# A graph, attention and expert network on one core: first expert layer scattered by token, key loads placed behind the first stores of scoring

## The reference, cut to what matters

```python
# layer 0, graph: attention over edges
x_l = x @ W_l + b_l;  x_r = x @ W_r + b_r
alpha = einsum(leaky_relu(x_r[dst] + x_l[src]), att) + log(edge_weight)
out = segment_softmax(alpha, dst) applied to x_l[src], summed by dst
...
# layer 0, experts: the two best of eight per token, summed without weights
logits = h @ Wg + bg
top2 = two largest experts of each token
y = sum over e in top2 of (gelu(h @ W1[e] + b1[e]) @ W2[e] + b2[e])
# layer 1: graph convolution (project, gather by src, sum by dst), attention, experts with capacity
```

## Time and profile before

| | us |
|---|---|
| median of three runs (5753.02 to 5766.75) | 5758.02 |
| the profiled execution | 5764.05 |
| its span in the trace | 5762.3 |
| planning (0 to 86.9) | 86.9 |
| projecting (to 248.9) | 162.0 |
| scoring (to 1395.4) | 1146.5 |
| normalising (to 1512.1) | 116.7 |
| aggregating, attention (to 2090.2) | 578.1 |
| routing of layer 0 (to 2339.1) | 248.9 |
| experts of layer 0 (to 2821.9) | 482.8 |
| combining (to 2990.7) | 168.8 |
| all of layer 1 (to 5762.3) | 2771.6 |

### The profile page before, as it was taken

One profiled execution on the slowest core, in us unless ns is written; L12 is line 12 of the kernel. 1 busy time (PEld: TensorE's weight loads), 2 busy tenths in 40 slices (PEclk: granted clock), 3 DMA queues, 4 the chain that ended last, 5 costly groups with the idle time before them and its releaser, 6 DMA issues. The chain is left out here.

```text
span 5762.3 us, 68520 instructions
## 1 busy us (share of the span) xinstructions
PE 3544.4 (62%) x13636; PEld 2691.9 (47%) x13637; DVE 2995.2 (52%) x6650; ACT 1002.2 (17%) x2108; POOL 3048.8 (53%) x2954
## 2 busy tenths in 40 slices
PE   3755556554399760599635555554555555583998
PEld 3633334333277550377534444443544545461665
DVE  5367777777899762144453444444333333442443
ACT  0022222221399510122110000000000000021111
POOL 1167777774288525100367777776777777503111
PEclk9867777776699875799755666665555555556999
DMA  5477777774288542521241111112111111122220
GB/s 199 96 208 231 234 231 229 236 230 148 88 272 271 171 158 72 166 64 64 79 114 32 32 33 32 33 33 42 32 33 32 32 33 33 24 74 83 95 74 31
DMA packets 430920, 630.36 MB, mean 109 GB/s; under 512 B 100204, under 2 KB 307838, under 8 KB 429383
## 3 DMA queue, kind: packets, MB, share of 16 engines
q1 hardware_dynamic: 298907, 375.58, 20.5%
q0 software_dynamic: 107056, 200.91, 14.7%
q10 hardware_dynamic: 24876, 53.00, 2.6%
HBM read 419.56 MB, written 222.20 MB: 111 GB/s over the span
## 5 line engine op out<-in xcount | busy, mean ns | idle before, releaser
L1846 POOL DMA_INDIRECT big<-t_d,src_tiles x1564 | 1493.0, 955 | 551.0 <-issue 463.0
L2069 PE MATMUL v_bank<-big,v_oh 128*128 x3328 | 682.9, 391 | 928.1 <-POOLq L1842 857.3
L2069 PEld LDWEIGHTS v_bank<-big,v_oh 128*128 128x128 f32 x3328 | 650.3, 299 | 1004.0 <-issue 1004.0
L642 POOL DMA_INDIRECT big<-xl_d,src_steps x832 | 833.2, 1001 | 302.6 <-issue 244.7
L1924 DVE TENSOR_TENSOR big<-big,v_bank 128x64 f32 x1664 | 367.7, 221 | 1148.4 <-PE v_bank L2069 914.3
L738 PE MATMUL se_z_ps<-big,se_oht 128*128 x1664 | 654.1, 553 | 482.0 <-DVE se_z L685 174.1
L738 PEld LDWEIGHTS se_z_ps<-big,se_oht 128*128 128x128 f32 x1664 | 424.6, 272 | 711.1 <-issue 623.8
L685 DVE TENSOR_TENSOR se_z<-se_z_ps,big 128x528 f32<-128x528 f32 x416 | 291.7, 701 | 353.9 <-DMA big<-xl_d,src_steps 284.2
L955 POOL TENSOR_TENSOR ae_v<-ae_v,ex 128x1792 f32<-128x1792 f32 x104 | 334.5, 3219 | 236.6 <-DMA ae_v<-xj_d 236.3
L996 PE MATMUL ae_bank<-ae_v,ae_oh 128*128 128x266 f32 x1664 | 402.9, 397 | 49.7 <-DVE big L980 37.1
L996 PEld LDWEIGHTS ae_bank<-ae_v,ae_oh 128*128 128x128 f32 x1664 | 310.1, 191 | 142.3 <-DVE big L980 53.3
(11 more groups left out here) (401 smaller groups left out, 5174.4 us busy)
## 6 DMA issues: line engine op xcount, KB each, us to landing
xj_d<-big SPq DMA_DIRECT2D x208, 528.0 KB, 3.2
ae_v<-xj_d SPq DMA_DIRECT2D x208, 528.0 KB
se_dlb<-dlr_d SPq DMA_DIRECT2D x104, 256.0 KB, 5.0
big<-t_d,src_tiles POOLq DMA_INDIRECT x1564
buf_d<-e_blank ACTq DMA_DIRECT2D x4, 4112.0 KB, 36.2
e_xs<-buf_d SPq DMA_DIRECT2D x106, 128.0 KB
y_d<-e_y SPq DMA_DIRECT2D x106, 128.0 KB
big<-xl_d,src_steps POOLq DMA_INDIRECT x832
```

The source lines that it names most:

```text
L642: nc.gpsimd.indirect_dma_start(half_of(u)[:, k, :], None, table, bass.IndirectOffsetOnAxis(ap=m.src[:, t:t + 1], axis=0)).then_inc(landed[ ...
L1846: nc.gpsimd.indirect_dma_start(rows[:, t % RING, :], None, table, bass.IndirectOffsetOnAxis(ap=m.srct[:, t:t + 1], axis=0)).then_inc(lande ...
L2069: last = nc.tensor.matmul(bank[u][:, k * MH:(k + 1) * MH], oh[:, u, k, :], of_block(rows, at[k]), start=True, stop=True)
```

## The change

In the planning stage the table reads are left out and made at the start of `project_nodes`; the nine weight loads go from SP in `project_nodes` to ACT in `edge_steps`, ahead of the zero fill. In scoring each of the first four stores is followed by four key loads, and TensorE reads the blocks of four steps at a time. The blank rows of `buf1_d` are written in `normalise_edges`, by SP, together with the padding rows of `y0_d`. A row of `buf0_d` has two more numbers: the token and its first expert. `experts0` compares the first expert with the tile's expert (`erow`) and so gets the row of `y0_d`, which now has two planes of NP = 6272 rows in token order; POOL scatters each tile of results there. Rows that hold no token carry 1e6 and are dropped. Combining reads both planes with plain loads, `m.back` is gone.

```diff
@@ edge_steps, SP and ACT
-                sp.wait_ge(stored, 64)
-                sp.dma_start(m.btab, m.btab_d[0:NS].rearrange("(a n) -> a n", a=1)).then_inc(stored, 16)
...
                 sp.wait_ge(floats, 4)
-                sp.dma_start(m.dlr_d.rearrange("(j p) e -> p j e", p=P), flb[:, :, :]).then_inc(stored, 16)
-                sp.wait_ge(stored, 128)
+                sp.dma_start(m.dlr_d.rearrange("(j p) e -> p j e", p=P), flb[:, :, :]).then_inc(rowed, 16)
+                sp.wait_ge(rowed, 16)
...
+                load_projections(act, m, a)
@@ score_edges, SP and PE
-                for c in range(CH):
-                    sp.dma_start(key[c * H:(c + 1) * H, :], kd[c].partition_broadcast(H)).then_inc(s["keys"], 16)
+                def load_keys(h, u, r):
+                    if isinstance(h, int) and h < 4:
+                        for c in range(h * CH // 4, (h + 1) * CH // 4):
+                            sp.dma_start(key[c * H:(c + 1) * H, :], kd[c].partition_broadcast(H)).then_inc(s["keys"], 16)
...
-                pipeline(sp, 2 * NG, 4, (0, load_locals), (4, store))
+                pipeline(sp, 2 * NG, 4, (0, load_locals), (4, store), (4, load_keys))
...
-                    blocks = blocks_of(nc, m, mybir.EngineType.PE, q * 2, 2)
+                    if v % 2 == 0:
+                        blocks[:] = blocks_of(nc, m, mybir.EngineType.PE, q * 2, 4)
@@ normalise_edges
+                for q in range(NE * CT // 16):
+                    sp.dma_start(slots[q], blank[:, :, :].to_broadcast([P, 16, RW])).then_inc(s["blanked"], 16)
+                for e in range(2):
+                    sp.dma_start(m.y0_d[e * NP + N:(e + 1) * NP, :], blank[0:NP - N, 0, 0:D]).then_inc(s["blanked"], 16)
@@ route, layer 0
+                    c.did(V.tensor_scalar(first[:, :], m.tmp1[:, :], float(NE), None, ALU.add))
...
-                    if v % 7 == 0 and layer == 1:
+                    if v % 7 == 0:
+                        for at, what in ((RW - 2, m.prob), (RW - 1, token)) if layer == 1 else ((TW - 2, token), (TW - 1, first)):
+                            V.tensor_copy(disp[:, v // 7, :, at], what[:, bass.ds(g * 7, 7)]).then_inc(s["t_ready"], 1)
@@ experts0
-                def store(j, u, r):
-                    sp.wait_ge(s["y_ready"], j + 1)
-                    sp.dma_start(m.y0_d[bass.ds(j * P, P), :], y[:, u, :]).then_inc(y_out[u], 16)
+                def index(j, u, r):
+                    dve.wait_ge(x_in[u], 16 * (r + 1))
+                    V.tensor_scalar(which[:, bass.ds(j, 1)], xs[:, u, TW - 1:TW], m.erow[:, bass.ds(j, 1)], float(NP),
+                                    ALU.not_equal, ALU.mult).then_inc(s["chosen"], 1)
+                    dve.wait_ge(s["chosen"], j + 1)
+                    V.tensor_tensor(idx[:, bass.ds(j, 1)], which[:, bass.ds(j, 1)], xs[:, u, TW - 2:TW - 1], ALU.add).then_inc(s["indexed"], 1)
...
-                pipeline(dve, T0, 2, (0, bias1), (1, turned), (2, bias2))
+                pipeline(dve, T0, 2, (0, index), (2, bias1), (3, turned), (4, bias2))
...
+                for j in range(T0):
+                    pool.wait_ge(s["indexed"], j + 1)
+                    pool.sem_inc(s["issued"], 1)
+                    pool.wait_ge(s["y_ready"], j + 1)
+                    nc.gpsimd.indirect_dma_start(m.y0_d, bass.IndirectOffsetOnAxis(ap=idx[:, j:j + 1], axis=0), y[:, j % 2, :], None,
+                                                 bounds_check=2 * NP - 1, oob_is_err=False).then_inc(y_out[j % 2], 16)
...
-                act.wait_ge(s["blank"], 2)
-                for q in range(NE * CT // 16):
-                    act.dma_start(slots[q], blank[:, :, :].to_broadcast([P, 16, RW])).then_inc(s["blanked"], 16)
@@ combine_and_project
-                            nc.gpsimd.indirect_dma_start(y[:, u, e, i, :], None, m.y0_d,
-                                                         bass.IndirectOffsetOnAxis(ap=idx[:, u, e, i:i + 1], axis=0))\
-                                .then_inc(y_in[u], 16)
...
+                def load(g, u, r):
+                    if at_least(g, 2):
+                        sp.wait_ge(s["used"], g - 1)
+                    for e in range(2):
+                        sp.dma_start(y[:, u, e, :, :], rows[e][:, bass.ds(g * G, G), :]).then_inc(y_in[u], 16)
```

More of the change, by code:

```diff
@@ L57 @@
 RW = 2 * D + 2
+TW = D + 2
 assert NS % CH == 0 and LAST < P and NB % 7 == 0
@@ L728, in _ @@
             def _(pe):
+                blocks = []
                 def expand(q, v, r):
@@ L759, in normalise_edges @@
         bank = [ctx.enter_context(nc.psum_tensor(f"ne_bank{i}", [P, 512], F32)) for i in range(4)]
-        s = {n: m.sem("ne_" + n) for n in "w ln logw turned back cols rowps rows colps exps exped unturned done chain".split()}
+        blank = sb("blank", [P, 1, RW])
+        s = {n: m.sem("ne_" + n) for n in "blank blanked w ln logw turned back cols rowps rows colps exps exped unturned done chain".split()}
         key, run = m.big1[:, 0:CL], m.big1[:, CL:2 * CL + 1]
@@ L1253, in route @@
         base, tiles, tint = sb("base", [P, NE]), sb("tiles", [P, NE]), sb("tint", [P, NE], I32)
-        trow = sb("trow", [1, T0])
         sf = sb("sf", [P, 2, NB])
-        disp = sb("disp", [P, 2, 7, D if layer == 0 else RW])
+        disp = sb("disp", [P, 2, 7, TW if layer == 0 else RW])
+        first = sb("first", [P, NB])
         token = sb("token", [P, NB])
@@ L1525, in load @@
                         sp.wait_ge(s["xt_made"], j - 1)
+                        sp.wait_ge(s["indexed"], j - 1)
                     sp.dma_start(xs[:, u, :], m.buf0_d[bass.ds(j * P, P), :]).then_inc(x_in[u], 16)
-                def store(j, u, r):
-                    sp.wait_ge(s["y_ready"], j + 1)
-                    sp.dma_start(m.y0_d[bass.ds(j * P, P), :], y[:, u, :]).then_inc(y_out[u], 16)
-                pipeline(sp, T0, 2, (0, load), (6, store))
-                for u in range(2):
-                    sp.wait_ge(y_out[u], 16 * T0 // 2)
+                pipeline(sp, T0, 2, (0, load))
             @block.vector
@@ L1656, in combine_and_project @@
         bank = [ctx.enter_context(nc.psum_tensor(f"cp_bank{i}", [P, 512], F32)) for i in range(6)]
-        s = {n: m.sem("cp_" + n) for n in ("indexed issued y0 y1 used stat chain weights var std xn_ready xt_made xt_ready "
+        s = {n: m.sem("cp_" + n) for n in ("y0 y1 used stat chain weights var std xn_ready xt_made xt_ready "
                                            "xt_stored h_made t_ready stored").split()}
@@ L1691, in store @@
                         .then_inc(s["stored"], 16)
-                pipeline(sp, NGR, 2, (0, store))
+                pipeline(sp, NGR, 2, (0, load), (2, store))
                 sp.wait_ge(s["xt_stored"], 16 * NGR)
@@ L2427, in build @@
         m.out = out
-        edge_steps(nc, m, a)
-        end_stage(nc, m)
-        for stage in (project_nodes, score_edges, normalise_edges, aggregate_edges, finish_attention):
+        with ExitStack() as proj:
+            projection_weights(nc, m, proj)
+            edge_steps(nc, m, a)
+            end_stage(nc, m)
+            project_nodes(nc, m, a)
+            end_stage(nc, m)
+        for stage in (score_edges, normalise_edges, aggregate_edges, finish_attention):
             stage(nc, m, a)
```

127 lines of the change are left out of this document (66 added, 61 removed).

## The result

| | before | changed |
|---|---|---|
| median, us | 5755.52 (5748.75 to 5766.75, 4 runs) | 5680.14 (5678.98 to 5688.89, 4 runs) |
| ratio | | 0.987, 95% interval 0.9851 to 0.9889 |
| span of the profiled execution, us | 5762.3 | 5686.8 |

The changed kernel is faster by 75.4 us, or 1.3% (64 to 86 us by the interval). Forecast was 5699, range 5668 to 5726: the time is in the range on the side that was likeliest, and 19 us under the forecast.

What follows compares the result with a forecast made beforehand. Barriers separate the stages, each bound by its last wait: POOL's gathers pace scoring, TensorE the first expert layer, an engine chain combining. Terms -2 -6.3 -8 +1 -29.5 +9.4 -11.5 -12.8 = -59.7 from 5758.02: forecast 5699, range 5668 to 5726.

Steps and rivals of the forecast that it cites:

- Part 1: End of planning: dlr_d's store issued right behind need_d's, -2 us; start of projecting: weights loaded a stage earlier, -6.3.
- the two bounds: End of planning: dlr_d's store lands alone by about 78 (gain 8 us) or after need_d at about 84 (gain 3).
- Part 2: Scoring: target loads ahead of the keys, four keys behind each of the first four stores; POOL's ninth half earlier, -8 us.
- The rule that I cited: Scoring's queue: descriptors are consumed in ring order within a queue, so stores wait for keys; near -8 us, not -20.
- bound of -20: Scoring: if stores slipped past the keys, POOL would only lose its waits for the first halves, -20 us.
- Part 3: Normalising stage: the fill of buf1_d moves there, hidden in a stage without DMA, 0 us.
- Part 4: Routing: one more small VectorE operation on the path, two more POOL waits per group, +1 us (0 to +3).
- Part 5: First expert layer: loop starts earlier without the fill, -29.5 us; loop unchanged; POOL's drain behind 106 scatters, +9.4.
- case C: First expert layer: a y buffer waits for its scatter, up to 5825 us, chance 0.04; 5740 to 5770, another 0.04.
- Part 6: Combining: plain loads replace gathers; first sum earlier, -11.5 us, and all later waits gone, -12.8.
- A: Expert layer's tail or scoring: scatters leave no drain (-8.7) or keys don't hold stores (-12 more): 5678 to 5690; chance 0.19.
- B: Scoring: keys and gathers hamper each other, +8 in place of -8, first stage ends no earlier: 5715 to 5720; chance 0.19.

Runs made afterwards that it cites:

- the second sample: Both kernels profiled once more, nothing altered: changed kernel 5680.75 us, ratio 0.9874; kernel before 5753.32 us, one run.
- the third run: Kernel before with only the blank rows of buf1_d moved from the first expert layer to the normalising stage: ratio 0.994.

## Why the prediction was right, and where it was off

**Part 1.** -2 forecast, -2.1; -6.3 forecast, -5.7. dlr_d's store was issued at 73 instead of 83 and the stage gained 2: it landed at 83.6, so that of the two bounds the later one held (landing at about 84, with need_d). The nine profiles of the new form end the stage between 84.2 and 87.8, the five of the old one between 85.8 and 86.8, so the 2 us are hardly more than their scatter.

**Part 2.** Right in its mechanism for most of the holes, too small in its size, and wrong in its lower bound. The holes ahead of halves 6 to 9 came as told, 9.2 to 11.5 us each where 5 to 12 were forecast, and the ninth half came at the old clock's 330 (80.9 us into the stage) where 331 was forecast. That it fits to 1 us is luck: this profile was the dearest of its kind. The others with keys in bursts behind the stores have 70.0 and 74.1, and 69.9 and 78.3 on the slower chips; by the means over all of them, against 91.0 to 93.2 in the old form, the term is some -17 and not -8. What was mis-sized is the time for four keys and a store, 16.7 us in the forecast: from the sixth half to the ninth POOL's halves came 15.3 us apart in this profile, 12.6 in the second sample and 12.0 with the keys alone. The rule that I cited, ring order within a queue, agrees with the trace: behind the sixteenth key a store took 44.0 us to land. What the forecast missed is that this order isn't what the waits are paid by. Without it, with the keys on the other queue, they are as long, because gathers and stores are slow beside the burst as well. And the bound of -20 for stores that are not held was not worked out from anything: the hole at the start was 49.1 us, and with the keys spread the ninth half comes 49 us earlier than before.

Rows 7 had part of it in view, half of the DMA share at 79 GB/s with keys alone. By the Trainium skill (DMA: Bandwidth & Descriptors, Why a DMA increments its semaphore by 16 and not by 1) a transfer is cut over at most 16 engines, over the largest number that divides the outer dimension on both sides, so a load onto eight partitions uses eight; the share of 0.49 and the eight packets of each load agree. That a gather or a store needs all sixteen and so waits for the keys on those eight is argued from this, not shown; a key load cut over sixteen was not tried. The remaining 7 us of scoring in the profiled pair were scatter.

**Part 3.** 0 forecast, +0.4 (second samples +1.2); the four transfers and POOL's memsets lie beside VectorE's scans.

**Part 4.** +1 forecast, +0.8.

**Part 5.** Start -29.5 forecast (28.6 to 31), -30.5 measured. The loop: "unchanged 4.11 us" was a mean over a hole. 431.6 / 105 is 4.11, but 427.5 / 105 is 4.07, and the difference is the late load beside the fill that the third run took away; -4.1, 0 forecast. The end: +9.4 forecast, +9.9, with a drain of 8.716 us where 106 x 0.082 gave 8.7. The price was right, and the law behind it holds only as far as it was used, up to 106 scatters; that it held just so far is luck. VectorE's index operations, the scatters and the y buffers cost nothing, as told: landing after 2.1 to 2.8 us, far from the 7.6 at which case C would begin.

**Part 6.** -24.3 forecast, -25.6: 143.2 us where 144 was forecast, no wait after the first.

**The rivals.** The time lies in A's span (5678 to 5690), but neither of A's reasons held: the drain was 8.7 us, and stores were held by keys. The keys cost less than forecast all the same. B named a mechanism that is there, keys and gathers that hamper each other (39.4 us to landing), but the size, +8, is out, and so is C.

Together: -59.7 forecast, -75.5 between the two profiled spans; the 15.8 us on top in the profiled pair are 9.0 in scoring, 4.6 in the expert layer (4.1 of it the hole), 1.3 in combining and 0.9 in small ones. The upper end of the range, 5726, doesn't come out of the terms: their upper bounds add to 5722 (-35.7 from 5758.02); the lower ones do add to 5667.

## What to carry to other kernels

A transfer that nobody needs soon should neither stand in front nor follow in bursts: spread one by one over the stretch that it may take, the same bytes here cost no hole in POOL's work on ScalarE's queue, and at most one of 5.6 us on SP's, while in bursts of four or eight they cost some 30 us on either. A mean time per iteration read from first to last hides a stall; look at the single gaps before calling a loop steady. And replacing gathers by plain loads is worth more than one profile shows if some chips run gathers slower.

## What was unexpected of the hardware

- Chips differ by 9% on this kernel (5755 against 6287 and 6328 us), nearly all of it in stages full of gathers: POOL idles 360 to 376 us of scoring there on issue in place of 240 to 248, the difference in single stops of 2 to 7 us.
- With sixteen key loads of 208 KB issued in a burst, a gather took up to 39.4 us to land with the keys on another queue (its median in the steady state is 3.6), and a store in the same queue as the keys took 44.0 us (median 3.2). Moving the keys from one queue to the other did not change what POOL waited in sum, 29.5 and 31.7 us.
- POOL's drain at a stage's end rises by 0.082 us per scatter to 8.72 us at 106, and with more scatters it falls: 7.08 at 128, 4.47 at 160. Behind 782 gathers it is 9.03.
